# Mixer products, x2's norm and turn, and the routing scatters at other places in a hand-ordered schedule

## The reference, cut to what matters

```python
x = _layernorm(x + _L0_attn_ref(x, ...))        # a state-space mixer: 4 heads of 64, state 32
x = _layernorm(x + _L0_xattn_ref(x, ctx, ...))  # cross attention, 16 heads of 8
x = _layernorm(x + _L0_ffn_ref(x, ...))         # 8 experts, each row goes to its best 2
# mixer:   M = scores * Lmat;  y = M @ Xc + C @ states_in + D * xs;  y = rms(y * silu(z)) @ W_out
# experts: weights, selected = top_k(x @ gate, 2);  rows sorted by expert, silu(h@w0)*(h@w1) @ wo, put back
```

## Time and profile before

| | us |
|---|---|
| median of 3 runs | 428.56 |
| lowest, highest | 424.75, 432.4 |
| the profiled execution | 421.96 |
| its span, first to last instruction | 420.6 |

### The profile page before, as it was taken

The page is one execution under the profiler, slowest core; times in us unless marked ns, Lnnn a source line. Parts: engine busy times, 40 slices in busy tenths (PEclk is TensorE's granted clock), DMA queues, the critical chain, the costliest instruction groups (busy, mean ns, idle before and its releaser), DMA issues.

```text
span 420.6 us, 8854 instructions
## 1 busy us (share of the span) xinstructions
PE 342.2 (81%) x2781; PEld 232.4 (55%) x2781; DVE 289.2 (69%) x832; ACT 235.5 (56%) x462; POOL 238.2 (57%) x354
## 2 busy tenths in 40 slices
PE   2999977888878788877869799868997999999700
PEld 1666645555434354434434345457876989989600
DVE  3555645888888998878787523376776777777535
ACT  1677544432667675464668676734535566566405
POOL 3660598754444462545389889556575544554624
PEclk9999999999999998999898855998999999999955
DMA  8933222625505040506235353201113211111063
GB/s 271 325 104 109 95 76 74 201 87 182 164 30 164 5 140 3 159 11 183 85 83 152 104 148 101 52 25 52 42 39 88 66 52 50 42 51 38 27 211 100
DMA packets 44156, 41.96 MB, mean 100 GB/s; under 512 B 4512, under 2 KB 38112, under 8 KB 44112
## 3 DMA queue, kind: packets, MB, share of 16 engines
q1 hardware_dynamic: 40976, 35.10, 27.7%
q0 software_dynamic: 2272, 4.69, 3.1%
q10 hardware_dynamic: 864, 1.61, 1.1%
HBM read 26.36 MB, written 14.75 MB: 98 GB/s over the span
## 4 chain that ended last, share of the span: by engine, by line
PE 44%; DVE 21%; POOL 20%; issue 9%; ACT 3%; DMA 2%; another core or an unknown queue 1%; DVEq 0%; POOLq 0%; ACTq 0%
PE banks L994 12%; DVE nm L1187 8%; POOL w_split L1694 6%; PE banks L1021 5%; POOL slots_dram L1682 4%; PE banks L691 4%; PE banks L1009 3%; PE banks L839 2%; PE banks L1022 2%; PE banks L748 2%; DVE ctx_in L1129 2%; PE banks L887 1%; PE banks L786 1%; POOL cs_wide L1607 1%
## 5 line engine op out<-in xcount | busy, mean ns | idle before, releaser
L1187 DVE TENSOR_REDUCE nm<-banks 128x4 f32<-128x1024 f32 x64 | 78.0, 1220 | 17.1 <-PE banks L830 12.2
L1498 ACT ACTIVATE probs_all<-banks 128x1024 f32<-128x1024 f32 x64 | 65.4, 1021 | 37.2 <-PE banks L839 30.4
L994 PE MATMUL banks<-w_split,scores_in 128*128 x234 | 65.3, 414 | 0.0
L839 PE MATMUL banks<-scores_in 32*128 32x256 f32 x256 | 36.0, 360 | 23.5 <-DVE nm L1187 13.6
L839 PEld LDWEIGHTS banks<-scores_in 32*128 32x128 f32 x256 | 22.1, 207 | 50.0 <-DVE nm L1187 23.9
L1327 DVE TENSOR_TENSOR ctx_in<-ctx_in,banks 128x512 f32<-128x512 f32 x39 | 26.8, 687 | 29.1 <-ACT ctx_in L1545 22.5
L994 PEld LDWEIGHTS banks<-w_split,scores_in 128*128 128x128 f32 x234 | 41.3, 191 | 8.0 <-issue 1.1
L887 PE MATMUL banks<-probs_all,vals 128*9 128x256 f32 x512 | 44.6, 424 | 1.1 <-ACT probs_all L1498 0.6
L1545 ACT ACTIVATE ctx_in<-banks 128x512 f32<-128x512 f32 x39 | 23.3, 598 | 38.1 <-PE banks L994 34.6
L1701 POOL DMA_INDIRECT y_dram<-x,scatter_u x39 | 38.4, 986 | 10.9 <-POOL x L1699 10.6
L1682 POOL DMA_INDIRECT slots_dram<-rows,place_u x32 | 31.9, 996 | 21.6 <-DVE count L1287 14.0
(11 more groups left out here) (222 smaller groups left out, 786.0 us busy)
## 6 DMA issues: line engine op xcount, KB each, us to landing
scores_in<-k_dram SPq DMA_DIRECT2D x32, 128.0 KB, 2.7
scores_in<-q_dram SPq DMA_DIRECT2D x32, 128.0 KB, 2.6
ctx_in<-in_L_ffn_w SPq DMA_DIRECT2D x16, 256.0 KB, 2.8
cs_wide<-cs_dram SPq DMA_DIRECT2D x14, 256.0 KB, 3.4
scores_in<-slots_dram SPq DMA_DIRECT2D x39, 65.0 KB, 1.8
k_dram<-split_qk SPq DMA_DIRECT2D x8, 256.0 KB, 2.5
q_dram<-split_qk SPq DMA_DIRECT2D x8, 256.0 KB, 2.3
ctx_in<-in_L_ffn_wo SPq DMA_DIRECT2D x8, 256.0 KB, 3.1
```

The costliest lines, as they stand in the source:

```text
L839: return TE.matmul(EXPS[:, i * BANK + k * S:i * BANK + (k + 1) * S], keys[rows_j, ring, r, k * P:(k + 1) * P], queries[rows_j, ring, r, :] ...
L994: m = TE.matmul(up_bank(i, j), xT[:, i % XT, xh, :], all_weights[:, c + j * FF:][:, bass.ds(expert_at[i], FF)], start=n == 0, stop=n == 2)
L1187: V.tensor_reduce(most, maxima_of(n).rearrange("p (j k q) -> p j k q", j=2, k=TPS), AX_X, ALU.max, negate=True).then_inc(s["nmax"], 1)
L1498: C.activation(probs(n).rearrange("p j k q -> p (j k q)"), EXPS, ACT.Exp, scale=SCALE).then_inc(s["probs"], 1)
```

## The change

- PE's part of `mix` is a stage apart from the sums (`mix_sums`, DVE and POOL, still lag 3). For tiles 0 to 7 it keeps lag 3 but comes first in `mixer_step`, ahead of the batch's stages. For tiles 8 to 15 the product with the state comes at lag 0 and the eight products at lag 1.
- `x2_norm` moves into `READY`, ahead of `rank_chosen`.
- `split_x2` moves behind `mixer_step`; the copy of the rows is a stage of its own, `copy_rows`, at lag 11 (8 for the last two batches).
- `place_chosen` issues one scatter a step, at lags 15 to 18, instead of four at lag 15. In `END_HALVES` the four stay together.
- Unread products: `split_x2` has one instead of two (none for batch 0), `rank_chosen` gets one for batches 0 to 5; the one in every eight steps moves from place 7 to place 3; steps 52 to 63 get one each, written to the bank of the maxima.

```diff
-TILE_LAGS = (('mix_square', 5), ('mix', 3), ('mix_matrix', 0), ('mix_exps', -1), ...)
+TILE_LAGS = (('mix_square', 5), ('mix_sums', 3), ('mix_matrix', 0), ('mix_exps', -1), ...)
 def mixer_step(n):
+    for t in range(NT):
+        state_lag, lag = (3, 3) if t <= FIRST_TILES else (0, 1)
+        if n == tile_step(t) + state_lag and t % TPS:
+            yield "mix_state", t
+        if n == tile_step(t) + lag:
+            yield "mix", t
...
-READY = ("rank_chosen", "gate_top", "turn_heads", "out_project", "divide")
+LATE = ("split_x2",)
+READY = ("x2_norm", "rank_chosen", "gate_top", "turn_heads", "out_project", "divide")
 AFTER = (
-    (lambda b: (("rank_chosen", b), ("place_chosen", b)), 15),
+    (whole("x2_norm"), 7),
+    (whole("rank_chosen"), 15),
+    *((half("place_chosen", i), 15 + i) for i in range(TOPK * TPS)),
     (whole("gate_top"), 9),
     (whole("choose"), 10),
     (whole("split_x2"), 8),
-    (whole("x2_norm"), 7),
+    (whole("copy_rows"), 11),
...
-SOONER = (10, 9, 9, 7, 6, 5, 4, 3, 2, 0)
+SOONER = (6, 10, *range(10, 10 + TOPK * TPS), 9, 9, 7, 8, 5, 4, 3, 2, 0)
...
-        yield from (stage for stage in after_attention(n) if stage[0] not in READY)
+        yield from (stage for stage in after_attention(n) if stage[0] not in READY + LATE)
         yield from mixer_step(n)
+        yield from (stage for stage in after_attention(n) if stage[0] in LATE)
...
-        if UNREAD_FROM <= n < 4 and n != 2:
+        if UNREAD_FROM <= n < 4 and n != 2 or n > ALL_MAXIMA:
             yield "unread_step", n
-        elif n % PAIRS_B == PAIRS_B - 1 and n < ALL_MAXIMA:
+        elif n >= 4 and n % PAIRS_B == 3 and n < ALL_MAXIMA:
             yield "unread_step", n
...
+                if n > ALL_MAXIMA:
+                    q.wait_ge(s["nmax"], NPAIR)
+                    TE.matmul(MAXIMA[:, BANK:BANK + S], ident, kv[:, 0:S], start=True, stop=True)
+                    return
...
+            def mix_state(t):
+                at, g = in_group(t)
+                q.wait_ge(s["y_sum"], t)
+                q.wait_ge(s["state"], t // TPS + 1)
+                TE.matmul(Y_SUMS[:, DI:2 * DI], bcT[at, g, 1, :], state[at, :], start=True, stop=True,
+                          tile_position=(at.start, 0)).then_inc(s["off_mm"], 1)
...
             def split_x2(b):
                 misc.wait()
-                if b < B - 2:
-                    unread(2)
+                if 0 < b < B - 2:
+                    unread(1)
...
                 misc.wait()
+                if b < B - 2:
+                    unread(1)
                 for t in range(TPS):          # rank_chosen
...
-            def place_chosen(b):
+            def place_chosen(b, i):
                 q.wait_ge(s["counted"], b + 1)
                 q.wait_ge(s["rows_x2"], b + 1)
-                for i in range(TOPK * TPS):
-                    G.indirect_dma_start(...)
+                G.indirect_dma_start(...)
```

More of the change, by code:

```diff
@@ L68 @@
 LAGS = (('load_queries', 12), ('query', 11), ('turn_x1', 10), ('mix_norm', 9), ('mix_residual', 7), ('mix_project', 7), ('turn_mixed', 6))
[L69 removed]
+TILE_LAGS = (('mix_square', 5), ('mix_sums', 3), ('mix_matrix', 0), ('mix_exps', -1), ('scale_inputs', -5), ('mask_decays', -3), ('load_sums', -10))
 ALL_MAXIMA = NPAIR - LEAD
@@ L181, with all_places @@
 COUNTED = PAIRS_B * FULL_BATCHES[0] + 1 + 15
+def all_places(b):
+    return [("place_chosen", b, i) for i in range(TOPK * TPS)]
 END_HALVES = {
-    0: (("silu_table",), ("weigh", NPAIR // 2 - 1, 0), ("split_x2", B - 2)),
+    0: (("silu_table",), ("weigh", NPAIR // 2 - 1, 0), ("split_x2", B - 2), ("copy_rows", B - 2)),
     1: (("weigh", NPAIR // 2 - 1, 1), ("evacuate", B - 1, 1)),
-    2: (("rank_chosen", B - 3), ("place_chosen", B - 3)),
+    2: (("rank_chosen", B - 3), *all_places(B - 3)),
     4: (("gate_top", B - 2), ("choose", B - 2)),
@@ L188 @@
     6: (("divide", B - 1, 1),),
-    7: (("rank_chosen", B - 2), ("place_chosen", B - 2)),
+    7: (("rank_chosen", B - 2), *all_places(B - 2)),
     9: (("turn_heads", B - 1),),
@@ L195 @@
     14: (("place_tiles", 1),),
-    15: (("split_x2", B - 1),),
+    15: (("split_x2", B - 1), ("copy_rows", B - 1)),
     17: (("gate_top", B - 1), ("choose", B - 1)),
-    19: (("rank_chosen", B - 1), ("place_chosen", B - 1)),
+    19: (("rank_chosen", B - 1), *all_places(B - 1)),
     21: (("count_tiles", 2),),
@@ L776, in mix @@
                 q.wait_ge(s["steps_a"], DEC_SET)
-                if k == 1:
-                    at, g = in_group(t)
-                    q.wait_ge(s["state"], b + 1)
-                    TE.matmul(Y_SUMS[:, DI:2 * DI], bcT[at, g, 1, :], state[at, :], start=True, stop=True,
-                              tile_position=(at.start, 0)).then_inc(s["off_mm"], 1)
                 q.wait_ge(s["mat"], t + 1)
@@ L1031, in tensor_program @@
                     front[stage](*at)
-            middle = dict(unread_step=unread_step, mix_matrix=mix_matrix, mix=mix, turn_mixed=turn_mixed, mix_project=mix_project,
+            middle = dict(unread_step=unread_step, mix_matrix=mix_matrix, mix_state=mix_state, mix=mix, turn_mixed=turn_mixed, mix_project=mix_project,
                           turn_x1=turn_x1, query=query, scores=scores, maxima_out=maxima_out, weigh=weigh,
@@ L1130, in mix_matrix, with mix_sums @@
                                 ALU.mult).then_inc(s["mat"], 1)
-            def mix(t):
+            def mix_sums(t):
                 b, k = divmod(t, TPS)
@@ L1356, in vector_program @@
                     front[stage](*at)
-            middle = dict(mix_matrix=mix_matrix, mix=mix, mix_residual=mix_residual, mix_norm=mix_norm,
+            middle = dict(mix_matrix=mix_matrix, mix_sums=mix_sums, mix_residual=mix_residual, mix_norm=mix_norm,
                           query=query, maxima=maxima, split_maxima=split_maxima, evacuate=evacuate,
@@ L1516, in split_x2, with copy_rows @@
                 C.activation(x2T[:, :], MISC[:, 0:S], ACT.Identity).then_inc(s["x2T"], 1)
+            def copy_rows(b):
                 q.wait_ge(s["x2"], TPS * (b + 1))
@@ L1564, in scalar_program @@
             middle = dict(mix_exps=mix_exps, mix_matrix=mix_matrix, mix_square=mix_square, turn_mixed=turn_mixed, turn_x1=turn_x1, query=query, maxima_out=maxima_out, exps=exps, evacuate=evacuate,
-                          turn_heads=turn_heads, split_x2=split_x2, split_weights=split_weights, silu_table=silu_table,
+                          turn_heads=turn_heads, split_x2=split_x2, copy_rows=copy_rows, split_weights=split_weights, silu_table=silu_table,
                           turn_x2=turn_x2, up=up, turn_hidden=turn_hidden, down=down)
@@ L1676, in choose @@
                 G.tensor_tensor(chosen[:, :, :], choice[:, 0], choice[:, 1], ALU.add).then_inc(s["chosen"], 1)
-            def place_chosen(b):
+            def place_chosen(b, i):
                 q.wait_ge(s["counted"], b + 1)
                 q.wait_ge(s["rows_x2"], b + 1)
-                for i in range(TOPK * TPS):
-                    G.indirect_dma_start(slots_dram[:, :], bass.IndirectOffsetOnAxis(ap=place_u[:, b % 2, i:i + 1], axis=0),
-                                         rows[:, b % 2, i // TPS, i % TPS, :], None).then_inc(a[f"slots{b % 2}"], 16)
+                G.indirect_dma_start(slots_dram[:, :], bass.IndirectOffsetOnAxis(ap=place_u[:, b % 2, i:i + 1], axis=0),
+                                     rows[:, b % 2, i // TPS, i % TPS, :], None).then_inc(a[f"slots{b % 2}"], 16)
             def split_weights(n):
@@ L1720, in pool_program @@
                 G.tensor_scalar(w_out[:, c, :], w_out[:, c, :], rms_w[:, c:c + 1], 0.5 * float(np.sqrt(DI)), ALU.mult, ALU.mult).then_inc(s["consts_g"], 1)
-            middle = dict(mask_decays=mask_decays, scale_inputs=scale_inputs, mix=mix, turn_mixed=turn_mixed,
+            middle = dict(mask_decays=mask_decays, scale_inputs=scale_inputs, mix_sums=mix_sums, turn_mixed=turn_mixed,
                           mix_residual=mix_residual, evacuate=evacuate, out_project=out_project, choose=choose, place_chosen=place_chosen,
```

2 lines of the change are left out of this document (removed).

## The result

The changed kernel took 433.52 us (median of 4 runs, 429.22 to 436.11) beside 429.36 for the kernel before: ratio 1.0162, 95% interval 1.0096 to 1.0227. Forecast were 427.7 us and a range up to 432.5. Measured again later, in 12 runs on one chip, it took 430.64 us (422.42 to 438.28) beside 428.57: ratio 1.0017 [0.9947, 1.0087]. So the first median lies 1.0 us above the range and the second inside it. The 12 runs of this one program lie 16 us apart, and their mean granted clock goes with them (422.42 us at 0.938, 438.28 at 0.890). Ratios are made from the less disturbed runs of both kernels, which are the faster ones, and medians from all runs. By the medians alone the change costs 1.0% the first time and 0.5% the second. Taken together it costs between nothing and 1.6%, where a gain of 0.2% was forecast.

The account below looks back on a forecast made before the run. DVE and PE, waiting for each other, bound steps 0 to 37, POOL steps 38 to 63. Terms -1.5 - 1.2 + 2.6 - 0.8 = -0.9 on 421.96 give 421.1 profiled, 427.7 us as median; range 420.5 to 432.5.

Parts of the forecast that it names:

- Products, tiles 8 to 15: Mixer products leaving place 7 for places 4, 5 and 1: DVE's waits for PE go, -1.5 us.
- The clock at 163.9: The fall to 0.50 behind 163.93, felt in step 23, was expected not to happen: -1.2 us.
- the turn put last: PE turns x2 behind a mixer product instead of ahead, with one filler less: nothing.
- x2's norm: Norm ahead of routing makes POOL's first scatter 0.9 us later in steps 40, 48 and 56: +2.6 us in all.
- the 1.1 us more: Extra over steps 40, 48 and 56 if the norm stands behind a whole weight piece of 1.27 us; not taken.
- One scatter a step: Spreading each batch's four scatters is the same work for POOL wherever they stand: nothing.
- Rival A: Scatters stop holding up PE's results in steps 26 and 35, and a second clock fall goes: -4.2 us more, 423.5, chance 0.25.
- the second fall of the clock: A fall behind the scatter waits, priced like the first at 1.2 us, counted only within Rival A.
- The late slots: Batch 4's last scatter moves from step 56 to 59, delaying SP's slot loads; POOL has about 7 us left: nothing.
- Fillers and stretch: Unread products in steps 52 to 63 bring the clock back within a few us of 239: -0.8 us.
- The stretch from the first weight piece to step 63: Steps 38 to 63, where POOL bounds: about 2 us longer than 60.1, named as a sign of being right.
- Rival C: Fillers in steps 52 to 63 run at 1.2 GHz and cost PE time: +12 us, 440, chance 0.08.

Follow-up runs that it names:

- products2: Kernel before with only the mixer products sooner and the unread product at place 3, repeated on another chip: 0.9944 of the kernel before.
- free2: Changed kernel with x2's norm on ACT, split of the maxima on ACT and POOL, batch 4's scatters together; a repetition: 0.9885 of the kernel before.
- a_act: Changed kernel with x2's norm at its new place but on ACT instead of DVE: 1.0061 of the kernel before.
- s_lock: Kernel before with products sooner, one scatter a step (batch 4's together), norm on ACT, split of the maxima on ACT and POOL: 1.0002 of the kernel before.
- b_scat: Kernel before with only one scatter a step, in all batches: 0.9987 of the kernel before.
- b_norm: Kernel before with only x2's norm ahead of the routing chain: 1.0182 of the kernel before.
- after: The changed kernel, whole change against the kernel before, first measurement: 433.52 us, ratio 1.0162.
- a_norm: Changed kernel with x2's norm behind the routing chain again: 0.9942 of the kernel before, though its median was 433.96 us beside 428.89.
- before: The kernel before, without the change: 429.36 us in the first measurement.
- b_prod: Kernel before with only the mixer products sooner and the unread product at place 3, first measurement: 0.9912 of the kernel before.
- a_lock: Changed kernel with x2's norm on ACT and the split of the maxima on ACT and POOL, nothing else undone: 0.9907 of the kernel before.
- a_four: Changed kernel with the four scatters of every batch in one step again: 1.0212 of the kernel before.
- p_turn: Kernel before with the mixer products sooner and x2 turned last in its step with one filler less: 0.9992 of the kernel before.
- a_b4: Changed kernel with only batch 4's four scatters together in step 56 again: 1.0162 of the kernel before.
- a_nofill: Changed kernel without the unread products of steps 52 to 63: 1.0110 of the kernel before.

## Why the prediction was wrong

**Products, tiles 8 to 15: right.** Steps -5, -1, 7 and 15 fell by 0.38, 0.61, 0.34 and 0.33 us, and step 23 from 4.76 to 3.93, where DVE no longer waited: 2.5 us with part of the clock's share, beside 1.5 forecast. Missed was the other side, 0.6 us at step -7, which holds the product that came to place 1. The part alone measured -0.6 and -0.9%, beside -2.7 us (0.6%) with its clock term. That these agree is in part luck, since the falls of the clock in the next paragraph were not in the sum.

**The clock at 163.9: right in its place, wrong in the sum.** Step 23 took 3.93 us in every kernel with the products. But in the changed kernel the clock fell at other places: at 119.8 and 130.2 for 3.4 us each, as in both runs of the products alone (119.4 and 129.6 in `products2`), and at 150.6 for 10.2 us, where steps 17 to 19 took 3.3 us longer. The long fall isn't the products' alone: `free2`, `a_act` and `products2`, with the same products, don't have it. It goes with the turn put last, a part that the prediction costed at nothing: all eight profiled executions with the turn last and the norm on DVE take 11.2 to 11.7 us for steps 17 to 19. Of the other twelve eight take 7.9, and four, `s_lock` with its turn in the old place among them, 8.8 to 12.7. So the turn's place isn't all of it, and no run separates it from the unread product that went with it. `b_scat` had two such stretches in instructions that are the kernel before's. A fall read from one execution was no term of a sum; it belonged into the range.

**x2's norm: the step that failed.** The term was 3 x 0.9, less what step 40 had waited already, = 2.6 us. POOL's waits for the count measured 5.7 instead of 0.3, that is 5.4 more. The 0.90 us in the earlier trace rows was taken as the price of the norm beside a piece. It was the price of beginning at 231.52, when 0.56 us of the piece (to 232.08) were left: its first operation stood that long, the second ran free. At the new place norm and piece are released by the same root, so the norm begins 0.07 us behind the piece every time and stands for all of it: 1.55 us, then the chain. That is 0.6 of the 0.9 us that each step lacked; the other 0.3 lie between the chain's end (233.66 + 0.16 = 233.82) and the scatter (234.12), which the sum left out. The duration was right for its moment, and the moment was what the edit moved. The Trainium skill (SBUF — State Buffer, "SBUF: two separate sides") says that the loser of the shared port pair, which DVE and GpSimd share, fully blocks until the other is done; the 1.1 us more that the prediction worked out by it were set aside in favour of the row. The trace agrees with the page: the norm's first operation lasts 1.29 us and ends 0.08 us behind the piece in three of three steps. By that 1.1 the sum would have been 3.7, still short of 5.4: the norm's second operation comes on top of the piece, and so do the 0.3. The conversion that stood behind four operations for 4.91 us goes further than the page's sentence. `b_norm` (1.0182) and `a_act` (waits gone) show the step by experiment.

**What no step of it had: the split of the maxima.** All that moved POOL's or DVE's order against each other also moved an operation of 0.18 us into or out of POOL's way. It cost 1.7 to 4.7 us a time in `after`, `a_norm`, `b_scat`, `a_act` and `b_norm`, and nothing in `before`, `b_prod` and `products2`. In `a_norm` PE idled 2.4 us meanwhile, in `a_act` 2.3, and in `a_norm`, `b_scat` and `a_act` the clock was at 0.50 for 10.2 us from there. That this is why undoing the norm alone didn't bring the median back fits the traces, and `a_lock`, with norm and split off DVE, bears it out; the split alone was not taken off the changed kernel.

**One scatter a step, costed at nothing: wrong twice, right at the end.** Rival A's mechanism did happen: steps 26, 34 and 42 lost 1.66, 1.35 and 1.46 us, and the second fall of the clock with them. With four scatters in one step they took 3.5 us or more in `a_four` (step 26 by its clock), `products2` and `p_turn`; but `b_prod` and `b_norm`, with the same burst, have 2.33 to 2.45 in steps 26 and 34. `b_prod` is the same program as `products2`, so the program doesn't decide it. Both without the stall ran on the one chip on which the kernel before took 422.8 us; whether it is the chip or the execution stays open, and with it how much of the ratios of that group carries over. The argument against A, that the spacing hardly changes, was wrong in its weight: one stage between the second scatter and the third is all there is (178.05, an operation of 0.65 us, 179.85), and the stall was gone. Rival A had 4.2 us for this; the step with the norm and the fall at 150.6 took them back. The late slots cost nothing that shows, as forecast (`a_b4`, `a_lock`), but PE had the last of them only at 271.11, 1.8 us before POOL's root ended (272.89) and not 7.

**Fillers and stretch.** The clock came back at 246.2, 17 us earlier than before, as expected. Of the 0.8 us that the term gave it, POOL's wait for DVE's sum shrank from 0.76 to 0.56 (1.31 without the fillers, in `a_nofill`), and new waits of POOL for ACT took 1.2; no gain shows between the changed kernel and `a_nofill`. The stretch from the first weight piece to step 63 was to be 2 us longer and was 7.4; the first piece was to come 2.7 us earlier and came 1.3. Rival C did not happen.

## What to carry to other kernels

The duration of such a DVE operation beside POOL (a norm, a conversion, a subtraction in SBUF) depends on when it starts: read where POOL's operation ends beside it before the number is moved to another place. If both are released by the same event, count the whole of POOL's operation, and look for small operations of DVE that a shift brings into POOL's way; taking them to ACT and POOL made a change that had lost up to 1.6% win 0.9 to 1.2%. A fall of the clock seen in one execution is no term of a sum, and a profile from one chip says little of a step on another.

## What the runs showed of the hardware

A conversion of 128x32 on DVE took 0.18 us alone, 2.02 behind two operations of POOL and 4.91 behind four: POOL took up its next operation each time before DVE's had its turn. A subtraction with two operands in SBUF stood in the same way (1.88 instead of 0.19). Beside a scatter alone the same conversion took from 0.18 us (`before`, 216.34) to 0.67 (`a_act`, 210.03, where it ended 0.04 us behind the scatter). The reductions of 128x1024 took 1.19 to 1.23 us all the same. At the end of bursts of four scatters ACT and DVE waited 0.9 to 3.7 us for something that the profile doesn't name: in ten of the thirteen profiled executions with such a burst before step 63 (not in `b_norm`, `b_prod` and `s_lock`), and in none of the seven with one scatter a step throughout. And one program had runs at 422 and at 438 us, with mean clocks of 0.94 and 0.89.
